# Sixteen token-tile loads issued from one queue instead of two, in a fused layer of a state-space branch and eight experts

## The reference

```python
xn = _layernorm(x, axis=-1)
x = x + attn(xn) + ffn(xn)

# attn (a recurrence over the sequence, state of 128)
u  = einsum('bsd,nd->bsn', x, Wi) + bi
sp = einsum('bsd,nd->bsn', x, Ws) + bs
state = tanh(state @ A.T + u_t @ B.T) + sp_t      # per step
y_t = state @ C.T
out = einsum('bsn,dn->bsd', ys, Wo) + bo

# ffn (8 experts, the best 2 per token, weights by softmax of the two logits)
logits = x @ router_weight
gate, up = halves of einsum('th,ehf->tef', x, gate_up_proj)
act  = (clip(up) + 1) * gate * sigmoid(1.702 * gate)
out  = sum over experts of w * (act @ down_proj)
```

## Time and profile before

| what | value |
|---|---|
| median of 3 runs | 1690.04 us |
| profiled execution | 1691.32 us |
| span of its slowest core (core 7) | 1689.8 us |
| spans of the 8 cores | 1683.5 to 1689.8 us |
| TensorE matmul busy | 1486.0 us (88%) |
| VectorE, ScalarE, GpSimd busy | 902.8, 560.5, 124.7 us |
| DMA queues: software (GpSimd), hardware (SyncE) | 59.90 and 13.11 MB |

### The profile page before, as it was taken

How to read it: one execution, slowest core, us unless ns; L and a number is a source line. 1 busy time by engine, 2 the same in 40 slices (tenths; PEclk the granted TensorE clock), 3 DMA queues, 4 the chain that set the end, 5 groups by cost and what they waited for, 6 DMA issues and landing times.

```text
span 1689.8 us, 25899 instructions; the slowest of 8 cores (1683.5 to 1689.8 us)
## 1 busy us (share of the span) xinstructions
PE 1486.0 (88%) x6998; PEld 669.1 (40%) x6998; DVE 902.8 (53%) x2133; ACT 560.5 (33%) x1013; POOL 124.7 (7%) x238
## 2 busy tenths in 40 slices
PE   0334788889999999999999999999999999999973
PEld 0112344413444444444444444444444444444432
DVE  0464566643466446644664366536653665366533
ACT  0442233450255125512551155115521552155200
POOL 2100000000000000000000000000000000000011
PEclk9966799958999999999999999999999999999995
DMA  4420021101222212221222122222222222222058
GB/s 71 131 76 1 8 32 26 26 13 26 32 39 38 45 27 41 41 44 26 40 41 44 28 38 38 44 32 39 38 44 32 39 38 45 32 39 38 15 103 219
DMA packets 36314, 74.66 MB, mean 44 GB/s; under 512 B 4864, under 2 KB 4864, under 8 KB 36176
## 3 DMA queue, kind: packets, MB, share of 16 engines
q0 software_dynamic: 32576, 59.90, 22.7%
q1 hardware_dynamic: 3600, 13.11, 2.1%
HBM read 120.10 MB, written 8.39 MB: 76 GB/s over the span
## 4 chain that ended last, share of the span: by engine, by line
PE 81%; DVE 6%; DMA 6%; issue 3%; ACT 3%; DVEq 0%; POOL 0%; ACTq 0%; POOLq 0%; SPq 0%
PE pb L287 26%; PE pb L867 25%; PE pb L277 24%; DMA xres<-xm 2%; DVE etu L313 1%; PE pb L737 1%; PE pb L742 1%; ACT et L326 1%; PE pb L480 1%; DMA xln<-xm 1%; DVE stat L396 1%; DMA y<-otm 1%; DVE acc L883 1%; PE pb L694 1%; DVE etg L318 1%
## 5 line engine op out<-in xcount | busy, mean ns | idle before, releaser
L277 PE MATMUL pb<-xn_fm,wgu 128*128 128x512 bf16 x2048 | 496.4, 383 | 1.7 <-ACT wbc L657 1.0
L287 PE MATMUL pb<-xn_fm,wgu 128*128 128x512 bf16 x2048 | 490.7, 380 | 0.0
L867 PE MATMUL pb<-act_w,wdb_ 128*128 128x512 bf16 x2048 | 450.0, 382 | 6.9 <-DVE acc L883 5.9
L883 DVE TENSOR_TENSOR acc<-acc,pb 128x512 bf16<-128x512 bf16 x256 | 176.1, 688 | 276.8 <-PE pb L867 274.2
L867 PEld LDWEIGHTS pb<-act_w,wdb_ 128*128 128x128 bf16 x2048 | 200.8, 98 | 253.4 <-issue 17.1
L277 PEld LDWEIGHTS pb<-xn_fm,wgu 128*128 128x128 bf16 x2048 | 197.8, 99 | 239.0 <-issue 16.8
L287 PEld LDWEIGHTS pb<-xn_fm,wgu 128*128 128x128 bf16 x2048 | 197.6, 98 | 230.1 <-issue 3.8
L307 ACT CAST etu<-pb 128x512 bf16<-128x512 f32 x224 | 131.4, 587 | 256.0 <-PE pb L287 256.0
L326 ACT ACTIVATE et<-etg 128x512 bf16<-128x512 bf16 x256 | 161.1, 629 | 66.3 <-DVE etg L318 32.4
L305 ACT CAST etg<-pb 128x512 bf16<-128x512 f32 x224 | 131.4, 587 | 91.0 <-PE pb L277 90.1
L321 DVE TENSOR_SCALAR etu<-etu,sbu 128x512 bf16<-128x512 bf16 x256 | 91.7, 358 | 110.9 <-ACT etu L307 105.2
(11 more groups left out here) (106 smaller groups left out, 534.5 us busy)
## 6 DMA issues: line engine op xcount, KB each, us to landing
wgu<-Wg POOLq DMA_DIRECT2D x64, 256.0 KB, 3.5
wgu<-Wu POOLq DMA_DIRECT2D x64, 256.0 KB, 3.5
wdb_<-Wd POOLq DMA_DIRECT2D x64, 256.0 KB, 3.5
y<-otm SPq DMA_DIRECT2D x16, 512.0 KB, 5.7
xln<-xm SPq DMA_DIRECT2D x8, 512.0 KB, 3.2
xln<-xm POOLq DMA_DIRECT2D x8, 512.0 KB, 3.6
xres<-xm POOLq DMA_DIRECT2D x16, 256.0 KB, 6.2
xln<-xw SPq DMA_DIRECT2D x1, 512.0 KB, 4.1
```

Of the source, the lines that this page charges most:

```text
L277: e.matmul(bg_[:, 0:STW], wgu[:, 2 * par, dc, :], rhs, start=(dc == 0), stop=(dc == NDC - 1)),
L287: e.matmul(bu2[:, 0:STW], wgu[:, 2 * par + 1, dc, :], rhs, start=(dc == 0), stop=(dc == NDC - 1)),
L867: e.matmul(bk[:, 0:STW], wdb_[:, par, ic, :], act_w[:, ic, stt * STW:(stt + 1) * STW], start=(ic == 0), stop=(ic == NDC - 1), skip_group_c ...
L883: e.tensor_add(acc[:, fc, stt * STW:(stt + 1) * STW], acc[:, fc, stt * STW:(stt + 1) * STW], bk[:, 0:STW]),
```

## The change

`emitLoad` issued the loads of even tiles on the queue of SyncE (`sy`) and those of odd tiles on the queue of GpSimd (`gp`). Now it issues all of them on the queue of SyncE. Semaphores, buffers and waits of each load are as before.

```diff
                     lxsem = "s_lx%d" % (tc % 2)
-                    lxv = dma("sy" if tc % 2 == 0 else "gp", lxsem,
-                              xln[:, par4], x_srcs[tc], wait=wl)
+                    lxv = dma("sy", lxsem, xln[:, par4], x_srcs[tc], wait=wl)
                     lnA[tc] = (lxsem, lxv)
```

## The result

The changed kernel took 1665.24 us (median of 9 runs) against 1691.49 us of the kernel before beside it; the ratio is 0.9848 (95% interval 0.9836 to 0.9859), so it is faster by 1.5%, about 26 us. The forecast was 1660.1 us, with a range of 1655 to 1666. Direction, cause and place came as forecast; one term of the sum was too small by some 3 us. The medians take in a few disturbed runs in which the cores of a die show a lower clock; the ratio leaves them out.

The account below looks back on a forecast made before the run. Tile 1's load, queued behind constants and weights, bounds the start. Last constant at 38.0 plus 7.2 puts projections at 45.2 instead of 75.12: 1690.0 - 29.9 = 1660.1 us, range 1655 to 1666 (8 in 10).

Parts of the forecast that it names:

- What bounds: Before the recurrence: tile 1's load sits behind constants and weights on GpSimd's queue; VectorE waits 44.7 us for it.
- Part one: Start of the columns: tile 1 summed at about 8 us instead of 52.03, 44 us earlier; tile 6 at 26.5.
- Part two: Column 5: first logits wait for the last constant, landed at 33.7 if undelayed; first projections start 7.2 us after its landing.
- Part three: Constants' loads: seven more tiles fly beside them and delay the last by 4.3 us (0 to 10.1), to 38.0.
- The sum: First projections at 45.2 instead of 75.12, 29.9 us earlier; nothing lost later, so 1690.0 - 29.9 = 1660.1 us.
- Undisturbed constants: Constants' loads: the last lands at 33.7 to 35.5 us despite the tiles; time 1655.8 to 1657.6; chance 0.16.
- VectorE holding up GpSimd: Constants' issue: five VectorE normalizations of 0.81 us hold up GpSimd, 4.1 us on top; time 1664.2; chance 0.05.
- No gain: Between 75 and 183 us: another wait loses the 30 us again before the recurrence; time about 1690; chance 0.03.
- the clock: Recurrence's start: TensorE's clock rises later, 0.84 us lost per group at the lower level; time 1694 and over; chance 0.03.
- Disturbed by nearly every tile: Constants' loads: each of seven tiles delays them by 1.3 to 1.44 us; time 1665 to 1666; chance 0.13.
- my likeliest case: Constants' loads: the tiles delay the last by 2 to 7 us; time 1657.6 to 1663; chance 0.60.

Follow-up runs that it names:

- the kernel that kept both queues: Kernel before, with the six weight loads issued on GpSimd's queue behind the tile loads instead of ahead of them: 1673.19 us, ratio 0.9898.
- unchained kernel: Changed kernel with each of the 18 constants issued without waiting for the one two before it: 1652.29 us, ratio 0.9778; run again, 1654.38 us, 0.9779.

## Why the prediction was right, point by point

- **What bounds.** Right. That place, not queue kind, held tile 1 is shown by the kernel that kept both queues and won 17 us.
- **Part one.** Right: second L395 at 7.98 (8 forecast), the sums of tile 6 at 26.60 (26.5). Behind tile 1 VectorE waited for no tile on any core (for tile 1 itself 0.93 us on core 4 and 0.20 on core 7): the single queue in order cost VectorE nothing.
- **Part two, the new gate.** Right, and the gate is shown from two sides: the logits wait for `sdm` by the trace, and without the chain this wait is gone. From the start of the logits to the projections 7.35 us passed, 7.1 by my sum.
- **Part three, the delay of the constants.** The mechanism was right, the size too small: I took 4.3 us, and measured were 7.4 over the cores (6.4 on core 7, from which I forecast: 31.52 to 37.90), so that the last constant landed near 40.6, not at 38.0. The step that failed is "I take three tiles in full, 3 x 1.44 = 4.3 us, and nothing for the other four". All seven count, with 1.06 us each on average instead of 1.44 for three. My thought that a tile beside a short, latency-bound load costs little was wrong: a load of 0.5 KB lost 1.3 us beside a tile. I had the same 1.3 us from `sAT` and did not apply it to the short ones. But that reading was weak: in the same trace `sCT`, as large as `sAT` and issued at 10.48 us, when tile 2 had landed, took as long with only the constant `sWiT` beside it (`sCT<-CT POOLq DMA_DIRECT2D x1, 32.0 KB, 3.6`). So it isn't shown how much of `sAT`'s 3.5 us was tile 2's doing, and the agreement that the prediction saw there is open; that the two queues' transfers slow each other is shown by `sbi` and by the table.
- **The sum.** 7.4 - 4.3 = 3.1 us of delay, 0.2 of the distance, and less than 1 us from the fact that the slowest core differs (an estimate), make 1660.1 into about 1664; measured were 1663.4 to 1665.2. That lies within the range, but near its upper end and outside the 1657.6 to 1663 to which I had given 0.60. It was the width of the range, not the size of my delay, that took it in.
- **Rivals.** Undisturbed constants: excluded by the table. VectorE holding up GpSimd: real, but 0.35 to 0.5 us on three of eight cores of the changed kernel and nothing on core 2, not 4.1 us. No gain, and the clock: neither came. The distance from the projections to the end is 1614.3 us, against 1614.7 before. The lower clock level (1.2 GHz, a granted clock of 0.50) held again for the first groups of the recurrence (1.87 us at 156.58), and the first group of 1.02 us started 5.5 us behind it, against 5.7 before. "Disturbed by nearly every tile" (0.13) had the mechanism that was measured: every tile counts. Its price, 1.3 to 1.44 us each, was too high, so that the kernel came out between my likeliest case and its 1665 to 1666, closer to the latter.

The unchained kernel beats both: ratio 0.978 in two separate comparisons, against 0.984 to 0.985 for the changed kernel.

## What to carry to other kernels

A long wait for a transfer at the start calls for a look at what its issuing queue was doing meanwhile; if it was waiting for others, the place in the queue is the price, and the profile gives the length of the wait (here 44.7 us, of which 26 came back). Before counting the gain, look for the wait that is invisible today because it has long been met (here a list of 18 constants), and put a time to it from the issue rows. What is moved early flies beside what was already early: count every such transfer against the chain it meets, the short loads too.

## What the runs showed of the hardware

- 512 KB of tile load in flight beside a chain of loads that wait for each other delayed the chain by 1.0 to 1.3 us each, from 2 to 16 of them. The chain's loads are of 0.2 to 256 KB, and the short ones lose too: `sbi`, 0.5 KB, took 3.6 us over the cores instead of 2.3.
- With 18 loads issued at once, each took long: `sWoT` 11.8 us to landing against 6.9 in the changed kernel, `sbi` 11.6 against 3.5. The two tiles on SyncE's queue that flew beside them took 9.7 and 10.1 us, where a tile of the changed kernel takes 4.0 in the median. By the trace, the waits for these and the later tiles lie between the 31 us expected for the projections and the 37 measured.
- GpSimd's issue of a load took 0.88 to 1.02 us instead of 0.53 on three cores of the changed kernel, and 0.83 without tiles 4 to 8, when VectorE's L434 (or L437) ran at the same time. In the unchained kernel the issue of `sdm` took 1.17 us, against 0.72 in the kernel before with unchained constants, where VectorE was idle; L434 took 0.88 there instead of 0.81.
